# Output projection of an fp8 attention layer: weights loaded into the context's memory, chunks in alternating order

## The chip, the cores and the metric

The kernel runs on one core of a Trainium2 chip. The metric is the time of one execution on the device in microseconds (us). The engines are TensorE (PE; its weight loads are PEld), VectorE (DVE), ScalarE (ACT), GpSimd (POOL) and SyncE (SP), which here issues all transfers.

## The reference, cut to what matters

The whole model has two layers, each with an attention over a wide context, a self-attention and a feed-forward part. The change touches the last step of the first one. There, 256 tokens of width 512 make 16 heads of self-attention (`core`) and 16 heads of attention over 4096 context rows (`xout`), each head 128 wide. The 32 heads are joined, divided by a smoothing vector, clamped, rounded to fp8 and multiplied by a weight matrix of 512 x 4096:

```python
core = _gqa(q, k, v).reshape(b, s, nh * d)
...
kvx = jnp.einsum('bsi,oi->bso', cond, w_kv_x)
...
xout = _gqa(qx, kx, vx).reshape(b, s, nh * d)
cat = jnp.concatenate([core, xout], axis=-1)
catq = _div_clamp_fp8(cat, proj_smooth)
return jnp.einsum('bsi,oi->bso', catq, wproj) * (proj_in_scale * proj_w_scale)
```

The result is added to `x`.

## The kernel before

The kernel is a sequence of stages. A stage owns its memory and semaphores, and every engine has its own instruction stream in it; at its end all engines meet at a barrier (line 79), and the memory is given back. Four stages matter here.

**Self-attention** writes heads 0 to 15 of `cat`, divided and clamped but not yet rounded to fp8. Meanwhile SP loads the context `ctxT` (128 partitions x 4 x 4096 values of fp32, 8 MB in all).

**Wide cross attention** goes over eight head groups and, in each, over eight blocks of the context. TensorE projects keys and values from `ctxT` (lines 406 and 418; in the last group the values are projected late, line 418), multiplies them with the queries (431) and weighs the values (441). A semaphore `s_vp` counts the late value projections, 2 for each of the last eight blocks. When they are done nothing reads `ctxT` any more. In the last steps VectorE adds up the sums of the softmax (634 and 635), divides, clamps and rounds to fp8 (lines 615 to 624, and `fp8_round`, lines 105 to 108), and writes heads 16 to 31 of `cat`. SP loads queries and weights and moves feed-forward units early in this stage; its last instruction waits for the last of these stores (line 370).

**Output projection** (`fp8_output_stage`) takes the 32 heads as eight chunks of four heads, in order 0 to 7. For a chunk:

- SP loads the raw weights, 128 x 2048 values of fp32 (1 MB), into one of three buffers `raw` (line 694), and waits for a buffer from the fourth load on.
- ScalarE copies them into `hi`, in the format that TensorE multiplies in one pass (line 704), and VectorE subtracts: `lo = raw - hi` (line 715). Both are rings of four buffers.
- Chunks 0 to 3 (self-attention) are rounded to fp8 by VectorE in four operations, into `lhs` (`fp8_round`). Chunks 4 to 7 have been rounded in the wide stage, and ScalarE only casts them into `lhs` (line 699), all four at the start of its stream.
- TensorE runs 16 matmuls of 128 x 512: for each of four heads and two halves of the tokens one with `hi` (line 730) and one with `lo` (732), all added into two accumulators.

TensorE waits for all four casts once (`s_q`) and then, chunk by chunk, for `lo`. VectorE does, in order, rounding 0, `lo` 0, rounding 1, `lo` 1 and so on to `lo` 3, then `lo` 4 to `lo` 7, waits for all products and updates `x` in two operations (line 720). A helper `link` lets VectorE wait for the operation that it has just issued, before it goes on; `dve.sem_inc` is an increment of its own behind it.

**Layer norm and causal attention** follow. Their weights are loaded by instructions that SP issues after the barrier.

Of the kernel before, what the change touches and what calls it, by code (L numbers as in the profile page):

```python
# [14 lines left out]
F32 = mybir.dt.float32  # L15
# [4 lines left out]
ALU = mybir.AluOpType  # L20
# [3 lines left out]
P = 128  # L24
TOK = 256
NT = TOK // P
DM = 512
KC = DM // P
D = 128
# [18 lines left out]
F_TILES = [(0, 128), (128, 128), (256, 96)]  # L48
FFN_LATE = [6, 22, 5, 7, 23] + [u + n for n in range(8, 16) for u in (0, 16)]
# [235 lines left out]
def wide_cross_attention_stage(nc, C, ctxT, s_ctx, w, s_w, wkv_dram, q_dram, vecs, inv_smooth, cat, units, early):  # L285
# [22 lines left out]
    with Stage(nc, "wide") as st:  # L308
# [32 lines left out]
        with nc.Block() as block:  # L341

            @block.sync
            def _(sp):
# [25 lines left out]
                sp.wait_ge(s_stored, 16 * FFN_EARLY)  # L370

# [300 lines left out]
def fp8_output_stage(nc, cat, w_dram, wscale, x):  # L672
# [3 lines left out]
    NRAW, NSPLIT = 3, 4  # L676
    with Stage(nc, "oproj") as st:
        power = st.sb("power", [P, CH * TOK], BF16)
        shifted = st.sb("shifted", [P, CH * TOK])
        lhs = st.sb("lhs", [P, 2 * NH, TOK], F32R)  # L680
        raw = [st.sb(f"raw{i}", [P, CH, DM]) for i in range(NRAW)]
# [3 lines left out]
        s_raw = [st.sem(f"raw_loaded{i}") for i in range(NRAW)]  # L685
        s_q, s_mm, s_hi, s_lo, s_dve = (st.sem(n) for n in ("rounded", "products", "high", "low", "dve"))
        with nc.Block() as block:

            @block.sync
            def _(sp):  # L690
                for c in range(NCH):
                    if c >= NRAW:
                        sp.wait_ge(s_lo, c - NRAW + 1)
                    sp.dma_start(raw[c % NRAW][:, :, :], w_dram[c]).then_inc(s_raw[c % NRAW], 16)

            @block.scalar
            def _(act):
                for c in range(NCH // 2, NCH):
                    act.copy(lhs[:, CH * c:CH * (c + 1), :], cat[:, CH * c:CH * (c + 1), :]).then_inc(s_q, 1)
                for c in range(NCH):  # L700
                    act.wait_ge(s_raw[c % NRAW], 16 * (c // NRAW + 1))
                    if c >= NSPLIT:
                        act.wait_ge(s_mm, c - NSPLIT + 1)
                    act.copy(hi[c % NSPLIT][:, :, :], raw[c % NRAW][:, :, :]).then_inc(s_hi, 1)

            @block.vector
            def _(dve):
                link = Chain(dve, s_dve).after
                for c in range(NCH):
                    if c < NCH // 2:  # L710
                        part = cat[:, CH * c:CH * (c + 1), :].rearrange("p a b -> p (a b)")
                        fp8_round(dve, link, part, power[:, :], shifted[:, :],
                                  lhs[:, CH * c:CH * (c + 1), :].rearrange("p a b -> p (a b)"))
                    dve.wait_ge(s_hi, c + 1)
                    link(dve.tensor_tensor(lo[c % NSPLIT][:, :, :], raw[c % NRAW][:, :, :], hi[c % NSPLIT][:, :, :].bitcast(F32),
                                           ALU.subtract))
                    dve.sem_inc(s_lo, 1)
                dve.wait_ge(s_mm, NCH)
                for t in range(NT):
                    link(dve.scalar_tensor_tensor(out=x[:, t, :], in0=acc[t][:, :], scalar=wscale[:, 0:1], in1=x[:, t, :],  # L720
                                                  op0=ALU.mult, op1=ALU.add))

            @block.tensor
            def _(pe):
                pe.wait_ge(s_q, NCH // 2)
                for c in range(NCH):
                    pe.wait_ge(s_lo, c + 1)
                    for j in range(CH):
                        for t in range(NT):
                            pe.matmul(acc[t][:, :], lhs[:, CH * c + j, t * P:(t + 1) * P], hi[c % NSPLIT][:, j, :],  # L730
                                      start=(c == 0 and j == 0), stop=False)
                            mm = pe.matmul(acc[t][:, :], lhs[:, CH * c + j, t * P:(t + 1) * P], lo[c % NSPLIT][:, j, :],
# [2371 lines left out]
```

## Time and profile before

| | |
|---|---|
| median of 3 runs | 2563.33 us (2561.7 to 2565.37) |
| profiled execution | 2560.87 us |
| its span | 2559.1 us |
| instructions | 31520 |
| TensorE busy | 2279.3 us, 89% |
| VectorE busy | 1786.6 us, 70% |
| ScalarE busy | 1193.7 us, 47% |
| GpSimd busy | 587.4 us, 23% |
| the output projection in the span | 1169.04 to 1217.83 us |

The profile is of one execution; its time is the span plus 1.8 us around it. Times inside the trace count from the start of the span. A matmul row's start is measured, and its end is modelled, so the pace of matmuls is read from one start to the next. In square brackets a row says how long the engine was idle before the instruction, and what released it; "DVEq L717" is the increment behind `lo`.

### The profile page before, as it was taken

The page shows a single profiled execution, that of the slowest core. Times are in us where ns is not written, and L with a number is a line of the kernel's source. Part 1 is how long each engine was busy: PE and PEld are TensorE (multiplying, and loading weights), DVE is VectorE, ACT ScalarE, POOL GpSimd, SP SyncE. Part 2 cuts the span into 40 slices and gives each one's busy share as a digit, 9 for nine tenths or more (in the row PEclk, how much of TensorE's full clock was granted, in tenths as well). Part 3 has the DMA queues.
Part 4 walks back from the last instruction along what each step waited for, and adds up shares of the span by engine and source line. Part 5 has one row for each costly group of instructions (what it writes and reads, how often), then busy time and mean ns, then how long its engine had stood idle before and what let it go on. Part 6 is the DMA issues. An engine that isn't in the chain of part 4 may idle for free. (4 is left out here: it accounts for less than half of the span.)

```text
span 2559.1 us, 31520 instructions
## 1 busy us (share of the span) xinstructions
PE 2279.3 (89%) x11472; PEld 1554.3 (61%) x11472; DVE 1786.6 (70%) x3422; ACT 1193.7 (47%) x1924; POOL 587.4 (23%) x435
## 2 busy tenths in 40 slices
PE   3779999999999999896897989788888779899998
PEld 2556666666666666564674456555556337677876
DVE  7856887777777778876896976666767754554444
ACT  4443466666566666633332114576766853211111
POOL 7810033334233333440000003323141300000000
PEclk9889999999999999998997999999999989899999
DMA  3331100000000100003544100000000013656661
GB/s 132 116 140 46 46 25 29 9 29 9 29 25 13 29 13 17 0 1 132 193 169 188 52 21 10 1 10 1 6 5 1 21 75 144 216 206 220 230 237 66
DMA packets 47622, 186.40 MB, mean 73 GB/s; under 512 B 6064, under 2 KB 10928, under 8 KB 37232
## 3 DMA queue, kind: packets, MB, share of 16 engines
q1 hardware_dynamic: 47472, 184.43, 20.0%
q8 instruction: 91, 1.49, 0.2%
q14 instruction: 59, 0.48, 0.1%
HBM read 174.71 MB, written 9.70 MB: 72 GB/s over the span
## 5 line engine op out<-in xcount | busy, mean ns | idle before, releaser
L406 PE MATMUL wide_a<-wide_w,ctxT 128*128 128x256 f32 (+1 forms) x2048 | 437.8, 367 | 2.8 <-POOL wide_eps L375 2.8
L406 PEld LDWEIGHTS wide_a<-wide_w,ctxT 128*128 128x128 f32 x2048 | 368.5, 191 | 76.5 <-issue 35.7
L388 POOL TENSOR_TENSOR wide_sums<-wide_sums,wide_s 128x512 f32<-128x512 f32 x224 | 301.3, 1345 | 461.8 <-ACT wide_s L536 448.6
L431 PE MATMUL wide_scores<-wide_q,wide_keysT 128*128 128x512 f32 x512 | 238.4, 604 | 12.5 <-ACT wide_s L532 12.5
L441 PE MATMUL wide_o<-wide_s,wide_values 128*128 128x512 f32 x512 | 233.8, 600 | 3.5 <-ACT wide_s L536 3.5
L532 ACT COPY wide_s<-wide_scores 128x512 f32<-128x512 f32 x256 | 148.4, 585 | 175.7 <-PE wide_scores L431 173.9
L1812 DVE TENSOR_REDUCE int_peaks<-int_a 128x1 f32<-128x1024 f32 x128 | 156.1, 1222 | 91.3 <-PE int_a L1535 90.1
L1535 PE MATMUL int_a<-int_keys,int_qrows 96*128 96x512 bf16 x512 | 151.8, 394 | 55.9 <-DVE int_peaks L1812 27.9
L1687 ACT ACTIVATE int_prob<-int_a,int_shift,int_qscale 128x1024 uint8<-128x1024 f32 x128 | 155.4, 1216 | 50.6 <-PE int_a L1535 50.1
L431 PEld LDWEIGHTS wide_scores<-wide_q,wide_keysT 128*128 128x128 f32 x512 | 87.9, 189 | 148.8 <-ACT wide_s L532 87.8
L594 DVE TENSOR_TENSOR wide_top<-wide_top,wide_s 128x512 f32<-128x512 f32 x240 | 165.6, 690 | 16.1 <-ACT wide_s L532 10.4
L2268 PEld LDWEIGHTS moe_bank<-moe_xb,moe_gate_up 128*128 128x128 f32 (+1 forms) x1536 | 162.0, 183 | 8.3 <-issue 8.3
L2268 PE MATMUL moe_bank<-moe_xb,moe_gate_up 128*128 128x96 f32 (+1 forms) x1536 | 162.6, 266 | 4.3 <-issue 4.3
L441 PEld LDWEIGHTS wide_o<-wide_s,wide_values 128*128 128x128 f32 x512 | 96.7, 192 | 100.2 <-issue 93.9
L607 DVE TENSOR_TENSOR wide_s<-wide_s,wide_peak_rows 128x2048 f32<-128x2048 f32 x64 | 146.8, 2294 | 0.8
L570 DVE BATCH_NORM_STATS2 wide_stats<-wide_keys 128x6 f32<-128x128 f32 x256 | 60.6, 278 | 110.9 <-ACT wide_values L514 108.4
L1446 PE MATMUL int_vp<-int_wk,ctxT_again 128*128 128x128 f32 x1024 | 126.6, 279 | 5.2 <-PEq L79 2.2
L1446 PEld LDWEIGHTS int_vp<-int_wk,ctxT_again 128*128 128x128 f32 x1024 | 122.7, 194 | 12.3 <-issue 4.0
L512 ACT COPY wide_keys<-wide_a 128x256 f32<-128x256 f32 x128 | 46.6, 364 | 174.3 <-PE wide_a L406 174.2
L536 ACT ACTIVATE wide_s<-wide_s 128x2048 f32<-128x2048 f32 x64 | 122.4, 1912 | 5.5 <-DVE wide_s L607 4.8
L1535 PEld LDWEIGHTS int_a<-int_keys,int_qrows 96*128 96x128 bf16 x512 | 37.0, 99 | 118.8 <-DVE int_peaks L1812 49.7
L2469 DVE TENSOR_REDUCE moe_coef<-moe_misc 96x1 f32<-96x4 f32 x32 | 5.1, 158 | 137.3 <-PE moe_misc L2277 137.3
(425 smaller groups left out, 4285.7 us busy)
## 6 DMA issues: line engine op xcount, KB each, us to landing
moe_gate_up<-hbm_m_gu SPq DMA_DIRECT2D x34, 1408.0 KB, 6.2
moe_down<-hbm_m_down_a SPq DMA_DIRECT2D x34, 512.0 KB, 6.9
causal_wqkv<-hbm_wqkv SPq DMA_DIRECT2D x8, 1536.0 KB, 6.6
ctxT<-hbm_ctxT SPq DMA_DIRECT2D x4, 2048.0 KB, 15.1
oproj_raw<-hbm_wproj SPq DMA_DIRECT2D x8, 1024.0 KB, 5.0
ctxT_again<-hbm_ctxT SPq DMA_DIRECT2D x4, 2048.0 KB, 21.6
wide_unit<-hbm_ffn_units SPq DMA_DIRECT2D x27, 256.0 KB, 2.7
ffn_early<-wide_unit SPq DMA_DIRECT2D x27, 256.0 KB, 2.0
```

The lines of the kernel that those rows point to most:

```text
L388: ins = pool.tensor_tensor(sums[0][:, :], before, part[:, j, :], ALU.add)
L406: mm = pe.matmul(a[h][:, j, cols], ctxT[:, kc, t * P:(t + 1) * P], w[g % 2][:, kc, cols], start=(kc == 0), stop=(kc == KC - 1))
L431: pe.matmul(sp_[j % 2][:, :], keysT[:, j, :], q[:, :], start=True, stop=True).then_inc(s_s, 1)
L441: mm = pe.matmul(o[g % 2][:, :], values[m % VR][:, j, :], s[m % SR][:, j, :], start=(c == 0 and j == 0), stop=(c == QPG - 1 and j == 3))
L532: act.copy(s[n % SR][:, j, :], sp_[j % 2][:, :]).then_inc(s_se, 1)
L594: link(dve.tensor_tensor(top[:, :], before, s[n % SR][:, j, :], ALU.max))
L607: dve.tensor_tensor(s[m % SR][:, :, :], s[m % SR][:, :, :], peak_rows[:, :].unsqueeze(1).to_broadcast([P, 4, COLS]), ALU.subtract).then_in ...
L1446: mm = pe.matmul(vp[:, t * P:(t + 1) * P], ctxT[:, kc, i * P:(i + 1) * P], wk[:, kc, :], start=(kc == 0), stop=(kc == KC - 1))
L1535: mm = pe.matmul(wide[n % 2][:, z * 512:(z + 1) * 512], qrows[0:3 * HD, h, t * P:(t + 1) * P], keys[0:3 * HD, h % HC, j * 512:(j + 1) * 51 ...
L1687: act.activation(prob[u % 4][:, p * 1024:(p + 1) * 1024], wide[n % 2][:, :], ACT.Exp, bias=shift[:, u % NU:u % NU + 1], scale=qscale[:, t, ...
L1812: dve.tensor_reduce(peaks[u % 2][:, p:p + 1], wide[n % 2][:, :], AX.X, ALU.max).then_inc(s_ad, 1)
L2268: mm = pe.matmul(dst[0:m, j, :], wgu[i][:, kc, z * EI + f0:z * EI + f0 + m], xb[q % 2][:, kc, e % BATCH, :], start=(kc == 0), stop=(kc == ...
```

## The change

Four things are edited.

1. The weights' memory. `raw` is a view of `ctxT` with eight places of 1 MB, one for each chunk. The two buffers of the wide stage's weights are freed before the projection stage; `ctxT` stays until its end.
2. The loads. A function issues four of them with no wait between. It is called at the end of SP's stream in the wide stage, behind a wait for the last value projection (`s_vp`), and again as SP's only work in the projection stage.
3. The order of chunks is 4, 0, 5, 1, 6, 2, 7, 3; the position in this order is `n`. ScalarE's cast of a chunk stands in front of its copy to `hi`; TensorE waits for each chunk's cast (`s_cast`) or rounding (`s_q`). `lhs` is eight tiles rather than one. The rings `hi` and `lo` have three buffers rather than four.
4. The waits. `lo` and the two updates of `x` no longer go through `link`; `lo` increments its semaphore itself. Each rounding is followed by an increment of its own (`s_q`).

```diff
--- before.py
+++ after.py
@@ -46,6 +46,7 @@
 TOPG = 3
 EG = 8
 F_TILES = [(0, 128), (128, 128), (256, 96)]
+OPROJ_ORDER = [4, 0, 5, 1, 6, 2, 7, 3]
 FFN_LATE = [6, 22, 5, 7, 23] + [u + n for n in range(8, 16) for u in (0, 16)]
 FFN_EARLY_UNITS = [n for first in (0, 16, 4, 20, 32, 36, 40, 44) for n in range(first, first + 4) if n not in FFN_LATE]
 FFN_EARLY = len(FFN_EARLY_UNITS)
@@ -282,7 +283,7 @@
                     assert chain.n == PER, chain.n
 
 
-def wide_cross_attention_stage(nc, C, ctxT, s_ctx, w, s_w, wkv_dram, q_dram, vecs, inv_smooth, cat, units, early):
+def wide_cross_attention_stage(nc, C, ctxT, s_ctx, w, s_w, wkv_dram, q_dram, vecs, inv_smooth, cat, units, early, loads):
 
 
 
@@ -368,6 +369,8 @@
                         if i + 2 < FFN_EARLY:
                             load_unit(i + 2)
                 sp.wait_ge(s_stored, 16 * FFN_EARLY)
+                sp.wait_ge(s_vp, 2 * (N - LATE))
+                loads(sp)
 
             @block.gpsimd
             def _(pool):
@@ -669,68 +672,64 @@
                     put(NG - 1, piece)
 
 
-def fp8_output_stage(nc, cat, w_dram, wscale, x):
+def fp8_output_stage(nc, cat, raw, s_raw, loads, wscale, x):
 
     CH = 4
     NCH = 2 * NH // CH
-    NRAW, NSPLIT = 3, 4
+    NSPLIT = 3
     with Stage(nc, "oproj") as st:
         power = st.sb("power", [P, CH * TOK], BF16)
         shifted = st.sb("shifted", [P, CH * TOK])
-        lhs = st.sb("lhs", [P, 2 * NH, TOK], F32R)
-        raw = [st.sb(f"raw{i}", [P, CH, DM]) for i in range(NRAW)]
+        lhs = [st.sb(f"lhs{c}", [P, CH, TOK], F32R) for c in range(NCH)]
         hi = [st.sb(f"hi{i}", [P, CH, DM], F32R) for i in range(NSPLIT)]
         lo = [st.sb(f"lo{i}", [P, CH, DM], F32R) for i in range(NSPLIT)]
         acc = [st.ps(f"acc{t}", [P, DM]) for t in range(NT)]
-        s_raw = [st.sem(f"raw_loaded{i}") for i in range(NRAW)]
-        s_q, s_mm, s_hi, s_lo, s_dve = (st.sem(n) for n in ("rounded", "products", "high", "low", "dve"))
+        s_cast, s_q, s_mm, s_hi, s_lo, s_dve = (st.sem(n) for n in ("cast", "rounded", "products", "high", "low", "dve"))
         with nc.Block() as block:
 
             @block.sync
             def _(sp):
-                for c in range(NCH):
-                    if c >= NRAW:
-                        sp.wait_ge(s_lo, c - NRAW + 1)
-                    sp.dma_start(raw[c % NRAW][:, :, :], w_dram[c]).then_inc(s_raw[c % NRAW], 16)
+                loads(sp)
 
             @block.scalar
             def _(act):
-                for c in range(NCH // 2, NCH):
-                    act.copy(lhs[:, CH * c:CH * (c + 1), :], cat[:, CH * c:CH * (c + 1), :]).then_inc(s_q, 1)
-                for c in range(NCH):
-                    act.wait_ge(s_raw[c % NRAW], 16 * (c // NRAW + 1))
-                    if c >= NSPLIT:
-                        act.wait_ge(s_mm, c - NSPLIT + 1)
-                    act.copy(hi[c % NSPLIT][:, :, :], raw[c % NRAW][:, :, :]).then_inc(s_hi, 1)
+                for n, c in enumerate(OPROJ_ORDER):
+                    if c >= NCH // 2:
+                        act.copy(lhs[c][:, :, :], cat[:, CH * c:CH * (c + 1), :]).then_inc(s_cast, 1)
+                    act.wait_ge(s_raw[n], 16)
+                    if n >= NSPLIT:
+                        act.wait_ge(s_mm, n - NSPLIT + 1)
+                    act.copy(hi[n % NSPLIT][:, :, :], raw[:, n, :, :]).then_inc(s_hi, 1)
 
             @block.vector
             def _(dve):
                 link = Chain(dve, s_dve).after
-                for c in range(NCH):
+                for n, c in enumerate(OPROJ_ORDER):
                     if c < NCH // 2:
                         part = cat[:, CH * c:CH * (c + 1), :].rearrange("p a b -> p (a b)")
-                        fp8_round(dve, link, part, power[:, :], shifted[:, :],
-                                  lhs[:, CH * c:CH * (c + 1), :].rearrange("p a b -> p (a b)"))
-                    dve.wait_ge(s_hi, c + 1)
-                    link(dve.tensor_tensor(lo[c % NSPLIT][:, :, :], raw[c % NRAW][:, :, :], hi[c % NSPLIT][:, :, :].bitcast(F32),
-                                           ALU.subtract))
-                    dve.sem_inc(s_lo, 1)
+                        fp8_round(dve, link, part, power[:, :], shifted[:, :], lhs[c][:, :, :].rearrange("p a b -> p (a b)"))
+                        dve.sem_inc(s_q, 1)
+                    dve.wait_ge(s_hi, n + 1)
+                    dve.tensor_tensor(lo[n % NSPLIT][:, :, :], raw[:, n, :, :], hi[n % NSPLIT][:, :, :].bitcast(F32), ALU.subtract).then_inc(s_lo, 1)
                 dve.wait_ge(s_mm, NCH)
                 for t in range(NT):
-                    link(dve.scalar_tensor_tensor(out=x[:, t, :], in0=acc[t][:, :], scalar=wscale[:, 0:1], in1=x[:, t, :],
-                                                  op0=ALU.mult, op1=ALU.add))
+                    dve.scalar_tensor_tensor(out=x[:, t, :], in0=acc[t][:, :], scalar=wscale[:, 0:1], in1=x[:, t, :],
+                                             op0=ALU.mult, op1=ALU.add)
 
             @block.tensor
             def _(pe):
-                pe.wait_ge(s_q, NCH // 2)
-                for c in range(NCH):
-                    pe.wait_ge(s_lo, c + 1)
+                for n, c in enumerate(OPROJ_ORDER):
+                    pe.wait_ge(s_lo, n + 1)
+                    if c < NCH // 2:
+                        pe.wait_ge(s_q, n // 2 + 1)
+                    else:
+                        pe.wait_ge(s_cast, n // 2 + 1)
                     for j in range(CH):
                         for t in range(NT):
-                            pe.matmul(acc[t][:, :], lhs[:, CH * c + j, t * P:(t + 1) * P], hi[c % NSPLIT][:, j, :],
-                                      start=(c == 0 and j == 0), stop=False)
-                            mm = pe.matmul(acc[t][:, :], lhs[:, CH * c + j, t * P:(t + 1) * P], lo[c % NSPLIT][:, j, :],
-                                           start=False, stop=(c == NCH - 1 and j == CH - 1))
+                            pe.matmul(acc[t][:, :], lhs[c][:, j, t * P:(t + 1) * P], hi[n % NSPLIT][:, j, :],
+                                      start=(n == 0 and j == 0), stop=False)
+                            mm = pe.matmul(acc[t][:, :], lhs[c][:, j, t * P:(t + 1) * P], lo[n % NSPLIT][:, j, :],
+                                           start=False, stop=(n == NCH - 1 and j == CH - 1))
                     mm.then_inc(s_mm, 1)
 
 
@@ -3065,6 +3064,7 @@
         s_ctx = nc.alloc_semaphore("ctx_loaded")
         q_dram = nc.dram_tensor("cross_queries", (P, NH, TOK), F32, kind="Internal").ap()
         with ExitStack() as cross:
+            weights = cross.enter_context(ExitStack())
             with ExitStack() as inner:
                 def sbi(name, shape, dt=F32):
                     return inner.enter_context(nc.sbuf_tensor(name, shape, dt, side="right"))
@@ -3073,7 +3073,7 @@
                 v = sbi("v", [P, NT, NG * D])
                 front_stage(nc, C, A, x, A, (ln2, in_scales, scales, wscale, vecs, smooth, inv_smooth), qT, q_dram, kT, v)
                 ctxT = cross.enter_context(nc.sbuf_tensor("ctxT", [P, KC, SC], F32))
-                w = [cross.enter_context(nc.sbuf_tensor(f"wide_w{i}", [P, KC, 2 * D], F32)) for i in range(2)]
+                w = [weights.enter_context(nc.sbuf_tensor(f"wide_w{i}", [P, KC, 2 * D], F32)) for i in range(2)]
                 s_w = [nc.alloc_semaphore(f"wide_w_loaded{i}") for i in range(2)]
                 def loads(sp):
                     sp.dma_start(w[0][:, :, :], A["wkvx"][0]).then_inc(s_w[0], 16)
@@ -3081,9 +3081,20 @@
                         sp.dma_start(ctxT[:, kc, :], A["ctxT"][:, kc, :]).then_inc(s_ctx, 16)
 
                 self_attention_stage(nc, C, qT, kT, v, inv_smooth, cat, loads)
+            raw = ctxT[:, :, :].rearrange("p k n -> p (k n)").rearrange("p (c j n) -> p c j n", c=8, n=DM)
+            s_raw = [nc.alloc_semaphore(f"wproj_loaded{n}") for n in range(8)]
+
+            def projection_loads(first):
+                def loads(sp):
+                    for n in range(first, first + 4):
+                        sp.dma_start(raw[:, n, :, :], A["wproj"][OPROJ_ORDER[n]]).then_inc(s_raw[n], 16)
+
+                return loads
+
             wide_cross_attention_stage(nc, C, ctxT, s_ctx, w, s_w, A["wkvx"], q_dram, vecs, inv_smooth, cat, A["ffn_units"],
-                                       early)
-        fp8_output_stage(nc, cat, A["wproj"], wscale, x)
+                                       early, projection_loads(0))
+            weights.close()
+            fp8_output_stage(nc, cat, raw, s_raw, projection_loads(4), wscale, x)
 
 
 _OUT = "out_dram"
```

## Rows read from the trace of the kernel before

**Rows 1.** The page: busy time of TensorE; the chain that ended last, by engine.

```profile
PE 2279.3 (89%) x11472; PEld 1554.3 (61%) x11472; DVE 1786.6 (70%) x3422; ACT 1193.7 (47%) x1924; POOL 587.4 (23%) x435
...
PE 13%; DMA 0%; issue 0%; ACT 0%; DVE 0%; SPq 0%; DVEq 0%
```

**Rows 2.** Windows: length, PE, PEld, DVE, ACT, POOL busy, clock, DMA share, GB/s.

```profile
1169.00:1184.00 15.00, 5.33 (x15) 4.29 (x16) 10.85 (x10) 10.02 (x8) 0.00 (x0) 0.54 0.74 280
1184.00:1196.20 12.20, 8.32 (x35) 5.97 (x33) 11.54 (x11) 4.58 (x3) 0.00 (x0) 1.00 0.52 174
...
1200.00:1216.30 16.30, 16.25 (x72) 13.11 (x70) 5.58 (x4) 3.83 (x2) 0.00 (x0) 1.00 0.17 69
...
1169.00:1218.70 49.70, 33.68 (x128) 26.34 (x128) 33.06 (x26) 19.14 (x12) 0.00 (x0) 0.83 0.46 169
```

**Rows 3.** Timeline of ScalarE in the stage: start, length, line, tiles.

```profile
1169.06 3.89 ACT L699 CAST oproj_lhs<-cat 128x1024 fp32r<-128x1024 bf16 x4 [15.35 <-PEq L79]
1174.16 1.90 ACT L704 CAST oproj_hi<-oproj_raw 128x2048 fp32r<-128x2048 f32 x1 [1.22 <-DMA oproj_raw<-hbm_wproj]
1176.88 1.90 ACT L704 CAST oproj_hi<-oproj_raw 128x2048 fp32r<-128x2048 f32 x1 [0.82 <-DMA oproj_raw<-hbm_wproj]
```

**Rows 4.** Timeline of VectorE in the stage.

```profile
1169.09 0.43 DVE L105 TENSOR_SCALAR oproj_power<-cat 128x1024 uint16<-128x1024 uint16 x1 [1.56 <-PEq L79]
...
1176.17 2.29 DVE L715 TENSOR_TENSOR oproj_lo<-oproj_raw,oproj_hi 128x2048 fp32r<-128x2048 f32 x1 [3.67 <-ACT oproj_hi L704]
1178.61 0.43 DVE L105 TENSOR_SCALAR oproj_power<-cat 128x1024 uint16<-128x1024 uint16 x1
...
1180.79 1.22 DVE L108 TENSOR_TENSOR oproj_lhs<-oproj_shifted,oproj_power 128x1024 fp32r<-128x1024 f32 x1
1182.05 2.29 DVE L715 TENSOR_TENSOR oproj_lo<-oproj_raw,oproj_hi 128x2048 fp32r<-128x2048 f32 x1
...
1193.82 7.17 DVE L715 TENSOR_TENSOR oproj_lo<-oproj_raw,oproj_hi 128x2048 fp32r<-128x2048 f32 x3
...
1216.29 1.54 DVE L720 SCALAR_TENSOR_TENSOR x_res<-oproj_acc,wscale,x_res 128x512 f32<-128x512 f32 x2 [8.61 <-PE oproj_acc L732]
1218.80 0.69 DVE L137 BATCH_NORM_STATS2 ln_stats<-x_res 128x6 f32<-128x512 f32 x1 [0.97 <-PEq L79]
```

**Rows 5.** Timeline of TensorE in the stage: eight of 128 matmuls.

```profile
1178.67 0.76 PE L730 MATMUL oproj_acc<-oproj_hi,oproj_lhs 128*128 128x512 f32 x1 [18.59 <-DVEq L717]
...
1183.01 0.40 PE L730 MATMUL oproj_acc<-oproj_hi,oproj_lhs 128*128 128x512 f32 x1
...
1184.45 0.50 PE L730 MATMUL oproj_acc<-oproj_hi,oproj_lhs 128*128 128x512 f32 x1
...
1187.99 0.39 PE L732 MATMUL oproj_acc<-oproj_lo,oproj_lhs 128*128 128x512 f32 x1
1190.34 0.50 PE L730 MATMUL oproj_acc<-oproj_hi,oproj_lhs 128*128 128x512 f32 x1 [1.96 <-DVEq L717]
...
1196.22 0.52 PE L730 MATMUL oproj_acc<-oproj_hi,oproj_lhs 128*128 128x512 f32 x1 [1.94 <-DVEq L717]
...
1199.95 0.42 PE L732 MATMUL oproj_acc<-oproj_lo,oproj_lhs 128*128 128x512 f32 x1
...
1215.87 0.39 PE L732 MATMUL oproj_acc<-oproj_lo,oproj_lhs 128*128 128x512 f32 x1
```

**Rows 6.** Waits of SP's queue from 1100 us: total, times, longest.

```profile
SPq L341 <- PEq L341: 153.1, 1, 153.1
```

**Rows 7.** Timeline of TensorE near the wide stage's end.

```profile
1147.75 3.73 PE L418 MATMUL wide_a<-wide_w,ctxT 128*128 128x128 f32 x32
```

**Rows 8.** The transfers into raw: time from issue to landing.

```profile
DMA to landing us min/median/max: 4.7/5.0/9.4
```

**Rows 9.** Timeline of VectorE in the wide stage.

```profile
1066.57 2.28 DVE L607 TENSOR_TENSOR wide_s<-wide_s,wide_peak_rows 128x2048 f32<-128x2048 f32 x1
1068.77 2.86 DVE L594 TENSOR_TENSOR wide_top<-wide_top,wide_s 128x512 f32<-128x512 f32 x4
```

## The prediction

> **What bounds the kernel now.** I began with the page. TensorE is busy 89% of the span, and the chain that ended last accounts for 13% of the span, all of it in the expert layer at the very end [rows 1]. So neither total nor chain says anything of the output projection; that has to be read from its own stretch.
>
> The windows of the stage come next [rows 2]. The stage lasts from 1169.0 to about 1217.9 us, 49 us or 1.9% of the span; nothing better than that is at stake. TensorE is busy 5.3 of the first 15 us, 8.3 of the next 12.2, and 16.25 of 16.3 in the last stretch. VectorE is the reverse: 10.9 of 15 and 11.5 of 12.2 early, 5.6 of 16.3 late. The reader is to see a stage in which first VectorE is the limit and TensorE waits, then TensorE is the limit and VectorE waits.
>
> The three timelines tell why. ScalarE spends 3.9 us on the four casts, then waits until 1174.16 for the first weights, whose transfer was issued when the stage began [rows 3]. The subtraction that makes `lo` waits for that copy and starts at 1176.17 [rows 4]. TensorE's first matmul is at 1178.67, 9.6 us into the stage [rows 5]. Chunks 0 to 3 each need a rounding and a subtraction: on VectorE the start of the second `lo` lies behind the first by 1182.05 - 1176.17 = 5.88 us, while TensorE needs 3.54 us plus one matmul at full clock (1184.45 to 1187.99), so TensorE idles some 2 us before 1190.34 and 1196.22. From there 80 matmuls run without a gap to 1215.87, their `hi` and `lo` having been made ahead. What sets the end is therefore VectorE's pace over the first four chunks, then 20.0 us of TensorE.
>
> **The change, part by part.** *Early loads.* Four of the eight 1 MB loads move from this stage to SP's queue at the end of the wide stage, behind a new wait for the last value projections. Those matmuls end at about 1151.5 [rows 7]. SP has by then nothing in its queue: it sits 153.1 us at the end of the wide block before TensorE ends [rows 6]. Nobody is queued behind the new wait, and nobody waits for SP before the barrier. Loads of this size landed in 4.7 to 9.4 us [rows 8] and, issued together, let their casts start 1176.88 - 1174.16 = 2.7 us apart, and the first cast started 5.1 us after the stage did [rows 3], so the four land by about 1151.5 + 5.1 + 3 x 2.7 = 1164.7. The first is wanted at 1170.0. Even at 9.4 us plus 8.1 us, the last is in by 1169.0. The cost of the move is nothing; the cover is the tail of the wide stage after 1151.5, and with that cover gone the first copy to `hi` would start at 1174.16 again. The bounds for a disturbance of the wide tail are 0 and small: VectorE's 0.43 us operations of the stage cost 0.43 us both at 1169.09 and at 1178.61, transfers under way [rows 4]. I take 0.
>
> *Late loads.* The other four are issued at the stage's start, without waits for a buffer, and land between 1174.2 and 1182.3 by the same reckoning. They serve positions 4 to 7, wanted from 1184 on. With weights always there in time, what is late next is VectorE.
>
> *Order 4, 0, 5, 1, 6, 2, 7, 3.* Roundings stay four and subtractions eight, but the two kinds of chunk alternate. This is the part that moves work: the surplus of VectorE in the first half and that of TensorE in the second now lie beside each other. Also the first chunk needs no rounding and the cast in front of it is one, not four.
>
> *Chained waits.* The subtraction no longer waits for itself and no longer needs a separate increment; each rounding gets a separate increment. Before, three subtractions in a row took 7.17 us, so 2.44 us from one to the next for 2.29 us of work, a gap of 0.15; the step inside a rounding has a gap of 0.03 to 0.04 [rows 4]. The difference, 0.11 us, I charge to each rounding for its new increment (bounds 0 and 0.11). A subtraction of the same shape without a wait is in the wide stage: 1066.57 to 1068.77, 2.20 us to the next start [rows 9]. So 2.44 becomes 2.20. The bounds are 2.20 and 2.44; I take 2.20, since the row has the same shape, operation and engine. The Trainium skill (VectorE: DVE Perf Modes, The DRAIN you can't avoid) says that operations with a semaphore after each run no slower than without; by that rule the pitch would stay at 2.44 and the gain below would be some 1.7 us smaller. The trace disagrees, with 2.44 against 2.20 us [rows 4, 9].
>
> **The sum.** ScalarE: cast at 1169.06; the next can start (3.89 - 1.04)/3 = 0.95 us later, 1170.0; the copy to `hi` takes 1.90, to 1171.9. VectorE starts the first `lo` 0.11 us behind it, as it did at 1176.17 behind 1176.06: 1172.0. From there it has no other wait: seven subtractions at 2.20 (15.4), four roundings at 3.44 (1178.61 to 1182.05) plus 0.11 (14.2), the last subtraction 2.29. Together 31.9 us, so the last `lo` is ready at 1203.9.
>
> Does TensorE keep up? Its first chunk can start at 1172.0 + 2.29 + 0.11 = 1174.4. The first ten matmuls before took 4.34 us, 0.43 each, at the lower level of the clock, 1.2 GHz (the stretch to 1184 was granted 0.54 in the mean) [rows 2], then 0.227 each, 15.92 us over the 70 steps from 1199.95 to 1215.87, at 2.4 GHz [rows 5]. That gives 5.7 us for the first chunk, at worst 6.9 if all 16 are slow: end 1180.1 to 1181.3. `lo` of the following positions is ready at 1180.1, 1182.3, 1188.0, 1190.2, 1195.9, 1198.1 and 1203.9. With 3.65 us a chunk TensorE starts them at 1180.2 (or 1181.3), 1183.9, 1188.1, 1191.8, 1196.0, 1199.7 and 1204.0. It waits some 0.5 us once in each pair and is never behind when the last `lo` comes; a slow start is absorbed.
>
> The rings go from four to three. ScalarE's copy for position n now waits for TensorE's chunk n - 3. Its tightest place is position 4: chunk 1 done at 1183.9 (1184.9 at worst), copy done by 1185.9 (1186.9), wanted by VectorE at 1187.9. Margin 1.0 us at worst. Cost 0, as long as the clock is up.
>
> End: last chunk 1204.0 + 3.54 + 0.39 = 1207.9, then the two updates of `x` take 1.54 or, without the wait between, about 1.4: 1209.4. Before, it was 1216.29 + 1.54 = 1217.8. The gain is 8.4 us: about 4.1 from the earlier first weights and fewer casts, the rest from alternation and the shorter pitch. The next stage starts by a barrier behind this (1218.80 for VectorE) and issues its own loads after it, so all moves by that amount.
>
> The profiled execution took 2560.87 us, span 2559.1; less 8.4 it gives 2552.5. The median of the runs lies 2.46 us above the profiled execution, so in terms of medians the forecast is 2563.33 - 8.4 = 2554.9, say 2555.0.
>
> **Rivals.**
>
> *A, the clock falls again and again.* The matmul row at 1196.22 follows a wait of 1.94 us, and up to 1199.95 nine matmuls take 3.73 us in place of 2.05: one fall costs 1.6 us [rows 5]. But the same wait before 1190.34 cost nothing, and the waits to come are 0.5 us. If it fell once in each pair, TensorE would need 128 x 0.227 = 29.1, plus 2.1 for the slow start, 6.4 for four falls and 1 for waits: end at 1213.0, a gain of 3.3 us, 2560.0. The Trainium skill (TensorE: Matmul & The Clock Gate, A second HAM failure mode: psum-queue depth-cycling) describes a kernel whose short, frequent idles between groups of matmuls made the clock oscillate; the change puts such idles where there was one long run. Chance 0.10.
>
> *B, slower.* The same place, carried to the end: the clock stays at its lower level. TensorE works from 1174.4 and must be done by 1216.3 to break even, 41.9 us; each slow matmul adds 0.2 us to 29.1, so from 64 slow matmuls of 128 the stage loses. All 128 slow: 54.7 us, end at 1229.3, 13 us late, 2576.3. For it: the stretch to 1184 had 0.54 of the clock. Against: that rose after 4.3 us of matmuls with no other help. Chance 0.03, and 0.02 for any other loss.
>
> *C, the loads come no earlier in effect* (the wait is released late, or the transfer waits for the barrier). Then the first copy starts at 1174.16 and all lies 4.1 us later: gain 4.3, 2559.0. Against it stand the 153 us of idle SP. Chance 0.06.
>
> *D, hidden anyway or given back later*: 2563.3. The next stage's first matmuls wait for loads issued in it, not at a fixed time, so this is unlikely: 0.06.
>
> **How the numbers follow.** The forecast case has 0.73. Its own range: gain 8.4, less 1.7 if the pitch stays 2.44, less 1.6 for one uncovered fall, plus 0.4 if the increments are free: 5.1 to 8.8 us; the three runs spread 1.8 us either way. From 2563.3 - 8.8 - 1.8 = 2552.7 to 2563.3 - 5.1 + 1.8 = 2560.0, which takes in A and C too; I widen the low end to 2552.0 for a fall of the clock that the kernel before has and the new one is spared. 0.2% is 5.1 us, about what a measurement can tell from no change. Faster by more: nearly all of the forecast case, a small part of A and C: 0.78. Within: 0.17. Slower: 0.05.
>
> **What would show it.** In the new profile: SP's first four loads at 1151.5; the first `hi` at 1170.0 and first `lo` at 1172.0; first matmul at 1174.4; subtractions 2.20 us before what follows them (2.44 would be the other bound); pairs of chunks 7.95 us apart on VectorE; TensorE waiting about 0.5 us per pair with a clock of 1.0 from 1181 on; `x` updated by 1209.4. Wrong would be: ScalarE waiting for TensorE at position 4 with VectorE behind it, TensorE without idle and a clock below 0.9, or a stage whose first VectorE operation starts later than 1169.09.

## The result, and the profile after

The changed kernel takes 2549.2 us in the median of 8 runs (2544.06 to 2554.91), the kernel before, timed in the same series, 2562.51. One of the eight runs of the kernel before took 9195.4 us; it counts in that median and not in the ratio, and without it the median is 2561.7. The ratio is 0.9957, with a 95% interval of 0.9944 to 0.9971: 11.0 us faster, between 7.4 and 14.3. The forecast was 2555.0 in a range of 2552.0 to 2560.0. The direction and the place of the gain are right, the time lies below the range.

The profiled span is 2543.0 us, 16.1 less than before. Only a part of that lies in the stage that was edited. First, its timelines after the change. ScalarE:

```profile
1165.14 1.04 ACT L698 CAST oproj_lhs<-cat 128x1024 fp32r<-128x1024 bf16 x1 [15.36 <-PEq L80]
1166.10 3.69 ACT L702 CAST oproj_hi<-ctxT 128x2048 fp32r<-128x2048 f32 x2
1169.69 1.04 ACT L698 CAST oproj_lhs<-cat 128x1024 fp32r<-128x1024 bf16 x1
1170.64 1.89 ACT L702 CAST oproj_hi<-ctxT 128x2048 fp32r<-128x2048 f32 x1
...
1180.16 1.91 ACT L702 CAST oproj_hi<-ctxT 128x2048 fp32r<-128x2048 f32 x1 [1.26 <-PE oproj_acc L731]
```

The first copy to `hi` starts 0.96 us into the stage, with no wait for weights; before, it was 5.1 [rows 3]. The first four of its loads were issued in the wide stage, behind the last value projection. TensorE, then SP, whose row covers all eight loads, the first at 1147.66 and the last four from 1165.12 on:

```profile
1143.84 3.73 PE L421 MATMUL wide_a<-wide_w,ctxT 128*128 128x128 f32 x32
1147.66 19.71 SPq L3090 DMA_DIRECT2D ctxT<-hbm_wproj  x8
```

The fourth load was issued at 1148.98, and the longest of the eight took 11.0 us to land, so the first four were in by 1160.0, 6 us before they were wanted. VectorE:

```profile
1168.02 2.29 DVE L713 TENSOR_TENSOR oproj_lo<-ctxT,oproj_hi 128x2048 fp32r<-128x2048 f32 x1 [4.42 <-ACT oproj_hi L702]
1170.23 0.42 DVE L106 TENSOR_SCALAR oproj_power<-cat 128x1024 uint16<-128x1024 uint16 x1
...
1173.78 4.49 DVE L713 TENSOR_TENSOR oproj_lo<-ctxT,oproj_hi 128x2048 fp32r<-128x2048 f32 x2
1178.19 0.42 DVE L106 TENSOR_SCALAR oproj_power<-cat 128x1024 uint16<-128x1024 uint16 x1
...
1197.65 2.29 DVE L713 TENSOR_TENSOR oproj_lo<-ctxT,oproj_hi 128x2048 fp32r<-128x2048 f32 x1
1204.00 1.41 DVE L716 SCALAR_TENSOR_TENSOR x_res<-oproj_acc,wscale,x_res 128x512 f32<-128x512 f32 x2 [4.06 <-PE oproj_acc L731]
1206.14 0.69 DVE L138 BATCH_NORM_STATS2 ln_stats<-x_res 128x6 f32<-128x512 f32 x1 [0.73 <-PEq L80]
```

From 1168.02 to the end of its last subtraction VectorE waits for nothing. Two subtractions take 4.49 us, so 2.20 from one to the next, and a rounding with its increment 3.55 (1170.23 to 1173.78). TensorE, six of its matmuls:

```profile
1170.37 0.80 PE L729 MATMUL oproj_acc<-oproj_hi,oproj_lhs 128*128 128x512 f32 x1 [14.21 <-DVE oproj_lo L713]
...
1173.94 0.41 PE L729 MATMUL oproj_acc<-oproj_hi,oproj_lhs 128*128 128x512 f32 x1
...
1184.08 0.50 PE L729 MATMUL oproj_acc<-oproj_hi,oproj_lhs 128*128 128x512 f32 x1 [0.39 <-DVE oproj_lo L713]
...
1192.04 0.50 PE L729 MATMUL oproj_acc<-oproj_hi,oproj_lhs 128*128 128x512 f32 x1 [0.41 <-DVE oproj_lo L713]
...
1200.00 0.50 PE L729 MATMUL oproj_acc<-oproj_hi,oproj_lhs 128*128 128x512 f32 x1 [0.37 <-DVE oproj_lo L713]
...
1203.57 0.39 PE L731 MATMUL oproj_acc<-oproj_lo,oproj_lhs 128*128 128x512 f32 x1
```

The first matmul comes 5.2 us into the stage, not 9.6 [rows 5], and the long run of 80 matmuls has gone. The waits that are left are of 0.2 to 0.4 us, always for `lo`. Windows of the stage, with the columns of [rows 2]:

```profile
1165.10:1180.10 15.00, 9.55 (x33) 7.47 (x34) 11.76 (x10) 10.25 (x7) 0.00 (x0) 0.71 0.70 281
1180.10:1204.00 23.90, 22.69 (x96) 17.41 (x94) 19.16 (x16) 8.59 (x5) 0.00 (x0) 1.00 0.00 0
```

The clock is at 2.4 GHz (1.00) throughout the second window. From the stage's first cast to the update of `x` it is 38.86 us, before 47.23: 8.37 less. From the first cast to the layer norm's first operation it is 41.00 against 49.74: 8.74 less. So the stage explains 8.7 of the 16.1 us. The remaining 7.4 us lie elsewhere, nearly all in code that nobody edited. The wide stage's first projection starts at 192.70, in the kernel before at 195.34: 2.6 us. The wide stage takes 1.3 us less, and the quantised attention, a stage of the second layer, 3.9 us less (599.5 for 603.4). The other stages together take 0.5 us more.

### The profile page after: what moved, and what is told of

Same layout as the page of the kernel before. It is cut to its first block and busy times, and to the rows that moved or that the text cites. A ratio compares the mean times of both kernels' runs of the same rounds, so it can differ in the third digit from the quotient of the medians.

```text
span 2543.0 us, 31519 instructions
## 1 busy us (share of the span) xinstructions
PE 2271.2 (89%) x11472; PEld 1548.0 (61%) x11472; DVE 1784.9 (70%) x3422; ACT 1193.7 (47%) x1924; POOL 587.2 (23%) x435
```

## The experiments

Two theories stand against each other. R: the change is worth the 8.7 us of its stage, and the rest is the spread of runs, which three runs had shown too small. M: the change also makes other stages faster, by its memory or its timing. Beside them stands the question within the stage: which edit brought how much. Below, "stage" is the time from the stage's first ScalarE instruction to the start of the update of `x`, and "wide" that from the first wide projection to the first ScalarE instruction of the projection stage, both from each kernel's timelines. A ratio compares a kernel with runs of the kernel before in its own series. The four from `same_before` to `late_loads` are one series, `old_order` to `rounded_ahead` another, on another chip, and `tail_rounds` a third; across series ratios are compared, not medians.

| kernel | median (runs) | ratio to before, 95% interval | wide | stage |
|---|---|---|---|---|
| before | 2562.51 (8) | | 973.7 | 47.23 |
| changed | 2549.2 (8) | 0.9957, 0.9944 to 0.9971 | 972.4 | 38.86 |
| `same_before` | 2559.4 (12) | 1.0000, 0.9988 to 1.0013 | 971.9 | 47.11 |
| `same_after` | 2549.69 (10) | 0.9961, 0.9949 to 0.9972 | 972.0 | 38.82 |
| `delay` | 2560.39 (12) | 1.0003, 0.9989 to 1.0016 | 974.3 | 48.15 |
| `late_loads` | 2555.88 (12) | 0.9983, 0.9970 to 0.9995 | 974.2 | 42.72 |
| `old_order` | 2553.48 (12) | 0.9971, 0.9961 to 0.9981 | 972.1 | 41.71 |
| `chained` | 2552.08 (7) | 0.9964, 0.9949 to 0.9980 | 972.5 | 40.59 |
| `round_first` | 2546.32 (6) | 0.9948, 0.9932 to 0.9965 | 971.7 | 37.65 |
| `rounded_ahead` | 2558.27 (12) | 0.9990, 0.9976 to 1.0004 | 984.8 | 35.81 |
| `tail_rounds` | 2548.65 (6) | 0.9952, 0.9939 to 0.9966 | 973.7 | 36.45 |

**`same_after` and `same_before`**: the two kernels once more, with no edit.

> The changed kernel again, unaltered. Its stage took 38.86 us from ScalarE's first cast (1165.14) to the update of x (1204.00), 8.36 less than the kernel before (1169.06 to 1216.29); 8.74 less to the first operation of the layer norm. Theory R: only the stage's 8.7 us are the change's, the rest of the difference of the profiled spans (16.1 us) is the spread of runs; then the stage takes 38.9 us again within 0.5, the ratio tends to 0.9966, and the two profiles of the same kernel differ by some us in stages that nobody edited (self-attention, quantised attention). Rival M: the rest (2 to 7 us) comes with the change; then the ratio stays at 0.9957 or lower and the wide stage again begins 2.6 us earlier, and the quantised attention again takes 4 us less.

> The kernel before against itself. Both theories: ratio 1.0000. It measures how far two sets of runs of one kernel lie apart, and its profile how far the stages of one kernel move between executions. Theory R needs movements of 2 to 4 us in single stages and a spread of runs of some 10 us; rival M expects the stages within 1 us of the kernel before's first profile.

The stage repeats within 0.12 us in either kernel. The rest of the program does not. In the second profile of the changed kernel the first wide projection starts 2.2 us later than in the first, though not a line differs:

```profile
192.70 7.58 PE L409 MATMUL wide_a<-wide_w,ctxT 128*128 128x256 f32 x34 [2.77 <-POOL wide_eps L378]
```

```profile
194.92 5.42 PE L409 MATMUL wide_a<-wide_w,ctxT 128*128 128x256 f32 x24 [2.77 <-POOL wide_eps L378]
```

Over all eleven profiles that start lies between 192.1 and 197.4 us. The quantised attention moves more. Its first ScalarE instruction and the next stage's first matmul, in the changed kernel:

```profile
1488.62 1.28 ACT L1623 ACT_TABLE_LOAD   x1 [7.44 <-PEq L80]
...
2088.10 1.22 PE L1941 MATMUL decay_pq<-xT,decay_wkv 128*128 128x256 f32 x2 [1.85 <-DMA decay_wq<-hbm_d_wq]
```

and in `same_after`:

```profile
1488.01 1.28 ACT L1623 ACT_TABLE_LOAD   x1 [7.26 <-PEq L80]
...
2092.84 1.65 PE L1941 MATMUL decay_pq<-xT,decay_wkv 128*128 128x256 f32 x3 [1.71 <-DMA decay_wq<-hbm_d_wq]
```

That is 599.5 and 604.8 us for one and the same kernel, so the 3.9 us that this stage seemed to gain lie within its own spread. Between the two profiles of the kernel before the wide stage differs by 1.8 us and this one by 1.9. M's forecasts, that stages stay within 1 us and that the two gains come again, are wrong.

The kernel before ran from 2550.64 to 2566.31 us in 33 runs, with a median of 2560.2, where the three runs shown ahead of the prediction had 2561.7 to 2565.37. In the two later series its medians were 2559.8 (28 runs) and 2559.77 (11). What goes with the spread is TensorE's granted clock. The 45 runs of the kernel before in this series, by the mean clock of each:

```
granted clock    runs   mean us   lowest    highest
0.963 to 0.967     11    2554.8   2550.64   2559.34
0.960 to 0.962     17    2559.4   2553.30   2562.39
0.957 to 0.959     17    2562.5   2559.07   2566.31
```

One stage shows how. Self-attention in `chained` and in `late_loads`, whose code is the same in it (windows, columns as in [rows 2]):

```profile
132.00:192.00 60.00, 45.91 (x192) 34.68 (x192) 36.31 (x96) 29.02 (x84) 10.11 (x23) 0.86 0.34 145
```

```profile
132.00:192.00 60.00, 47.18 (x182) 35.86 (x183) 34.15 (x93) 28.52 (x83) 11.19 (x24) 0.78 0.35 149
```

With a granted clock of 0.86 TensorE got 192 matmuls done in these 60 us, with 0.78 only 182; the wide stage starts at 192.13 in the one and at 197.41 in the other. About 1.3 of these 5.3 us lie ahead of the stage, which begins at 130.43 and at 131.71. The two profiles of the changed kernel fit in: 0.86 and 192.70, 0.83 and 194.92. Why the clock was granted less in one execution than in another no run shows.

**`delay`**: the gain handed back inside the stage.

```diff
                 dve.wait_ge(s_mm, NCH)
+                for _ in range(4):
+                    link(dve.tensor_tensor(lo[0][:, :, :], raw[:, 0, :, :], hi[0][:, :, :].bitcast(F32), ALU.subtract))
```

> The changed kernel with four more linked subtractions (2.33 us each) on VectorE in front of the update of x, about 9.3 us of waiting and nothing else: the stage is then 0.6 us longer than in the kernel before. Theory R: ratio to the kernel before 1.0002, within its interval. Rival M: still 2 to 7 us faster, 0.9973 to 0.9992. x is the same.

```profile
1210.59 9.27 DVE L716 TENSOR_TENSOR oproj_lo<-ctxT,oproj_hi 128x2048 fp32r<-128x2048 f32 x4 [4.04 <-PE oproj_acc L733]
1219.90 1.41 DVE L718 SCALAR_TENSOR_TENSOR x_res<-oproj_acc,wscale,x_res 128x512 f32<-128x512 f32 x2
```

The insertion took 9.3 us and the ratio is 1.0003. With the stage's gain cancelled nothing of the change can be seen; the interval reaches from 2.8 us faster to 4.1 us slower. That is the clearest evidence for R: it excludes all but the lowest end (2 us, 0.9992) of what M forecast. The profiled execution of `delay` is also a warning: taken alone, its 2567.19 us lie 6 us above the profiled execution of the kernel before.

**`late_loads`**: the early loads taken back.

```diff
                 sp.wait_ge(s_stored, 16 * FFN_EARLY)
-                sp.wait_ge(s_vp, 2 * (N - LATE))
-                loads(sp)
...
-                    for n in range(first, first + 4):
+                    for n in range(8):
```

> The changed kernel with all eight loads issued at the stage's start, none in the wide stage. My account: the first copy to hi waits for its weights until 5.1 us into the stage in place of 0.96, and all behind it is 4.1 us later; the gain over the kernel before falls from 8.7 to 4.6 us (ratio 0.9982). Rival: the early loads are worth nothing, since the casts and VectorE fill that time; then the stage stays 8.7 us shorter.

```profile
1171.63 1.04 ACT L696 CAST oproj_lhs<-cat 128x1024 fp32r<-128x1024 bf16 x1 [15.36 <-PEq L80]
1176.44 1.90 ACT L700 CAST oproj_hi<-ctxT 128x2048 fp32r<-128x2048 f32 x1 [3.76 <-DMA ctxT<-hbm_wproj]
```

The copy waits 3.76 us for the transfer, and the stage takes 42.72 us, 3.86 more than the changed kernel's. The early loads are worth that.

**`old_order`**: early loads and free subtractions, but chunks 0 to 7.

```diff
-OPROJ_ORDER = [4, 0, 5, 1, 6, 2, 7, 3]
+OPROJ_ORDER = [0, 1, 2, 3, 4, 5, 6, 7]
...
-                        pe.wait_ge(s_q, n // 2 + 1)
+                        pe.wait_ge(s_q, c + 1)
...
-                        pe.wait_ge(s_cast, n // 2 + 1)
+                        pe.wait_ge(s_cast, c - NCH // 2 + 1)
```

> The changed kernel with the chunks in order 0 to 7; early loads and unchained waits stay. My account: VectorE rounds and subtracts for each of the first four chunks, 3.55 + 2.20 = 5.75 us from one lo to the next, so the first matmul is at 6.0 us of the stage and the fourth chunk can begin at 23.2; from there 80 matmuls take 18.2 us. The update of x begins 41.8 us into the stage, 43.4 if the clock falls once as in the kernel before, against 38.86: 2.9 to 4.5 us of the gain are the order's. Rival: with weights there early the order is worth under 1 us, since TensorE is the bound either way.

```profile
1180.22 0.50 PE L729 MATMUL oproj_acc<-oproj_hi,oproj_lhs 128*128 128x512 f32 x1 [0.18 <-DVE oproj_lo L713]
1185.98 0.50 PE L729 MATMUL oproj_acc<-oproj_hi,oproj_lhs 128*128 128x512 f32 x1 [1.82 <-DVE oproj_lo L713]
1191.75 0.50 PE L729 MATMUL oproj_acc<-oproj_hi,oproj_lhs 128*128 128x512 f32 x1 [1.82 <-DVE oproj_lo L713]
```

The two idles of 1.8 us are back. The stage takes 41.71 us, so the order brings 2.85 us. The clock did not fall behind these idles: the matmuls after them start 0.23 us apart. The rival, under 1 us for the order, is out.

**`chained`**: the wait and the increment back behind each `lo`.

```diff
-                    dve.tensor_tensor(lo[n % NSPLIT]...).then_inc(s_lo, 1)
+                    link(dve.tensor_tensor(lo[n % NSPLIT]...))
+                    dve.sem_inc(s_lo, 1)
```

> The changed kernel with the helper's wait and the separate increment put back behind each lo. My account: the step from a lo to what follows goes from 2.20 to 2.44 us, seven times, and VectorE sets the end: the update of x begins 1.7 us later, 40.5 us into the stage. The rule that a semaphore behind an operation costs nothing: 38.9 as before.

```profile
1173.52 4.73 DVE L713 TENSOR_TENSOR oproj_lo<-ctxT,oproj_hi 128x2048 fp32r<-128x2048 f32 x2
1178.40 0.43 DVE L106 TENSOR_SCALAR oproj_power<-cat 128x1024 uint16<-128x1024 uint16 x1
```

Two subtractions take 4.73 us and what follows starts 4.88 after the first: 2.44 each. The stage takes 40.59 us, so the free subtractions bring 1.73 us, seven times 0.25. `chained` puts two things back at once, the wait for the operation itself and the increment of its own; in the changed kernel `lo` still raises a semaphore, and goes at 2.20. The rule of the Trainium skill (VectorE: DVE Perf Modes, The DRAIN you can't avoid) that a semaphore after each operation costs nothing fits that increment, and not the pair that `chained` puts back. The rows part the pair: in a rounding, where only the wait stands between two operations, the next one starts 0.03 to 0.04 us after the end of the last, behind a free `lo` it starts 0.09 us before the end shown (2.20 for 2.29), and a separate increment adds 0.11 us (3.55 for 3.44). By this estimate the wait costs about 0.13 us and the increment 0.11.

Each taken from the changed kernel alone, the early loads, the order and the free subtractions bring 3.86 + 2.85 + 1.73 = 8.44 us, and the whole stage gained 8.37: little is left for the casts and the rings.

**`round_first`**: chunk 0 rounded while VectorE waits for the first `hi`.

```diff
...
+                round_chunk(0)
                 for n, c in enumerate(OPROJ_ORDER):
-                    if c < NCH // 2:
...
+                    if 0 < c < NCH // 2:
+                        round_chunk(c)
```

> The changed kernel with chunk 0 rounded at the very start, in the time in which VectorE waits for the first hi. My account: first lo 3.55 us into the stage in place of 2.9, so the first matmul is 0.7 us later; but VectorE has 3.55 us less on the rest, and TensorE becomes the bound: 6.0 + 29.1 + 2.1 (slow start) + 0.4 = 37.6, 1.3 us less than 38.86. Rival: the ring of three stalls ScalarE and the end stays at 38.9.

The stage takes 37.65 us, 1.21 less than the changed kernel's. TensorE is now the limit: its first matmul is 5.93 us into the stage, and from there it runs without a wait. The ring of three does make ScalarE and behind it VectorE wait, by 0.4 and 1.3 us, but does not stall TensorE.

**`rounded_ahead`**: all of self-attention's heads rounded in the wide stage.

```diff
                 for n in range(N + LAG + 1):
+                    if n % QPG == 6:
+                        e = n // QPG
+                        if e < NG:
+                            own = cat[:, 2 * e:2 * e + 2, :].rearrange("p h n -> p (h n)")
+                            fp8_round(dve, link, own, power[:, :], out[:, :], own)
...
-                    if c >= NCH // 2:
-                        act.copy(lhs[c][:, :, :], cat[:, CH * c:CH * (c + 1), :]).then_inc(s_cast, 1)
...
+                    act.copy(lhs[c][:, :, :], cat[:, CH * c:CH * (c + 1), :]).then_inc(s_cast, 1)
...
```

> The changed kernel with the first 16 heads rounded in the wide stage, two heads each in eight of VectorE's gaps (in place, 2.1 us each), only casts left for ScalarE, and the copy to hi ahead of the cast. My account: VectorE has only the eight subtractions, the first lo is at 2.0 us and the first matmul at 4.4 us of the stage; TensorE is the bound: 4.4 + 29.1 + 2.1 + 0.4 = 36.0, 2.9 us less than 38.86, and the wide stage, bound by TensorE, costs nothing. Rival: the eight roundings of 2.1 us delay what TensorE waits for in the wide stage, up to 2 us each, and the kernel is slower than the changed one by up to 13 us.

The stage gains what was expected, 35.81 us, and the wide stage pays for it: 984.8 us against 971.7 to 974.3 in all others, 1.5 us for each of the eight roundings. My account failed there. VectorE in the middle of the wide stage:

```profile
612.13 0.61 DVE L106 TENSOR_SCALAR wide_power<-cat 128x512 uint16<-128x512 uint16 x1
612.77 1.31 DVE L107 TENSOR_SCALAR wide_power<-wide_power 128x512 bf16<-128x512 bf16 x1
614.11 1.70 DVE L108 TENSOR_TENSOR wide_out<-cat,wide_power 128x512 f32<-128x512 bf16 x1
615.85 0.69 DVE L109 TENSOR_TENSOR cat<-wide_out,wide_power 128x512 bf16<-128x512 f32 x1
616.58 0.48 DVE L573 BATCH_NORM_STATS2 wide_stats<-wide_keys 128x6 f32<-128x128 f32 x2
```

GpSimd at the same time:

```profile
609.53 5.74 POOL L391 TENSOR_TENSOR wide_sums<-wide_sums,wide_s 128x512 f32<-128x512 f32 x4 [8.67 <-ACT wide_s L539]
```

The rounding took 4.4 us, not 2.1, and the statistics of the next keys stand behind it. The three stretched operations lie beside GpSimd's additions (609.53 to 615.27) and the last one, at its usual 0.69, does not. The first of the eight roundings is the control: it comes before GpSimd's first addition and takes 2.0 us. Its second operation:

```profile
270.25 0.29 DVE L107 TENSOR_SCALAR wide_power<-wide_power 128x512 bf16<-128x512 bf16 x1
```

Six of the others took 4.4 us and the last, beside GpSimd throughout, 6.1. The Trainium skill (SBUF — State Buffer, Who interferes with whom) names such a conflict of VectorE with GpSimd over a shared port; the trace agrees, with 1.31 us for an operation of 0.29. On TensorE the delay shows as idle time in the wide stage, in the changed kernel and then in `rounded_ahead`:

```profile
PE wide_scores L434 <- ACT wide_s L535: 12.5, 15, 3.1
```

```profile
PE wide_scores L434 <- ACT wide_s L535: 20.9, 19, 3.1
```

That is 8.4 of the 12 us; the rest was not traced. Whether roundings of 2.1 us in these gaps would have been free was not tried.

**`tail_rounds`**: chunk 0 alone, in the two gaps at the wide stage's very end, and the copy to `hi` ahead of the cast.

```diff
+                    if n >= N + LAG - 1:
+                        e = n - (N + LAG - 1)
+                        own = cat[:, 2 * e:2 * e + 2, :].rearrange("p h n -> p (h n)")
+                        fp8_round(dve, link, own, power[:, :], out[:, :], own)
                     if n - LAG >= (NG - 1) * QPG and n - LAG < N:
                         add(n - LAG)
...
-                    if c >= NCH // 2:
+                    if c == 0 or c >= NCH // 2:
...
```

> The changed kernel with chunk 0 rounded in place in the two gaps that VectorE has in the last two steps of the wide stage (3.24 and 4.01 us idle in the trace, 2.1 us of rounding put into each), its cast left to ScalarE, and each copy to hi ahead of the cast. My account: both gaps end with a wait for something else, so the wide stage keeps its length (its first projection to the next stage's first instruction 972 to 974 us in seven profiles); the first matmul is at 4.4 us of the stage, and TensorE sets the end at 4.4 + 29.1 + 2.1 + 0.4 = 36.0, 2.9 us less than 38.86. Ratio to the kernel before 0.9955. Rival: work in VectorE's gaps is paid in full, as the eight roundings cost 12 us in rounded_ahead; then the wide stage is 4 us longer and the kernel 1 us slower than the changed one, 0.9970.

```profile
1158.38 0.69 DVE L109 TENSOR_TENSOR cat<-wide_out,wide_power 128x512 bf16<-128x512 f32 x1
1159.77 3.36 DVE L618 RECIPROCAL wide_out<-wide_rows 128x512 f32<-128x512 f32 x1 [0.69 <-PE wide_rows L479]
```

VectorE still waits 0.69 us for the sums after the second rounding, and waits 1.08 us after the first, so neither delays what follows it; wide, at 973.7 us, lies within the 971.7 to 974.3 of the other kernels. The stage takes 36.45 us, 0.5 more than expected and 2.4 less than the changed kernel's. The excess lies in the first chunk, which took 6.3 us for 5.8 in the changed kernel: twelve of its matmuls went at the slow pace of 0.43 us, not eight. Of the versions that leave the wide stage alone or nearly so, this one has the shortest projection stage; in runs it cannot be told from the changed kernel or from `round_first`, whose intervals overlap its own.

## Why the prediction was right in the stage and wrong in the range

- *Early loads land in time, at no cost*: right. SP issued them from 1147.66 on, as the last value projection ended, and wide is no longer with them (972.4 and 972.0) than without (974.2 in `late_loads`). I put 4.1 us on the first copy's earlier start, fewer casts included; `late_loads` measured 3.86.
- *The order* makes VectorE's pace the limit throughout: right. It waited for nothing after 1168.02. `old_order` took 41.71 us for a forecast of 41.8.
- *2.44 becomes 2.20, and 0.11 us for each rounding's increment*: right, 2.20 and 3.55 us; `chained` confirms the price. The sentence that the trace disagrees with the rule on semaphores went too far: the 2.44 us hold a wait and a separate increment, the 2.20 an increment on the operation itself.
- *TensorE keeps up, the ring of three costs nothing*: right; the first chunk took 5.75 us for 5.7. That a slow start is absorbed shows in `delay`: its first chunk took 6.55 us, and its last matmul began 38.42 us into the stage, as in the changed kernel (38.43).
- *The end*: 38.86 us from the stage's start, for 1207.9 - 1169.06 = 38.8. The two updates and the way to the layer norm gave 0.37 us more (1.41 for 1.54 us, then 0.73 us of waiting for 0.97), so the stage's gain is 8.74 for 8.4.
- *Rival A and B*, the clock: it stayed at 1.00 from 1180 on. *Rival C* is what `late_loads` builds: 4.3 us of gain forecast, 47.23 - 42.72 = 4.5 measured. *Rival D*, a gain hidden or given back later, is refuted by the ratio of the changed kernel; `delay` adds that time in this stage reaches the end: its 9.3 us moved the ratio from 0.9961 (`same_after`) to 1.0003, which is 10.8 us, with intervals of some 3 us either way.
- *What failed* is the step "the three runs spread 1.8 us either way", and with it the base of 2563.33. The kernel before spreads 8 us either way, and its median over 33 runs is 2560.2. The changed kernel's 8 runs spread over 10.9 us, and their median fell 2.8 us under the range. Of the 5.8 us between forecast (2555.0) and median (2549.2) the base accounts for 3.1 us (2563.33 less 2560.2) and the stage's larger gain for 0.3; the remaining 2.3 or so are the spread of eight runs or the remainder below, and no run parts the two. That the profiled execution (2560.87) lay below all three runs was a sign of this spread, and the prediction made nothing of it. It widened the low end instead for a fall of the clock that the new kernel is spared; but that fall lies before the 1216.29 from which the gain of 8.4 us was reckoned, and was counted already.

Open is a small remainder. Seven of the nine ratios of changed kernels lie 1 to 3.4 us below what their stage times give (0.9957 for 0.9966, `round_first` 0.9948 for 0.9961), each within its interval; `delay` and `late_loads` lie within 0.5 us of it. Four of the seven were compared with the same 28 runs of the kernel before, so they are not four witnesses. An effect of 1 or 2 us outside the stage is neither shown nor excluded.

## What to carry to other kernels

Where one engine is the limit in a stage's first half and another in its second, alternate the two kinds of work before making either faster; read both timelines and lay the surpluses side by side. Memory whose last reader ends before the stage does can take the next stage's first loads, and the price of being late is read from the first wait for a transfer. For an effect below 0.5%, read the edited stage in the trace, where it repeats to 0.1 us, and take the spread of the whole program from many runs, not from three.

## What the runs showed of the hardware

An idle of 1.8 us on TensorE did not lower the clock in `old_order`, twice, and one of 1.96 us in the kernel before did not, while the next one there, of 1.94 us, did [rows 5]. `same_before` fell at the same place, behind 1.97 us:

```profile
1194.96 0.51 PE L730 MATMUL oproj_acc<-oproj_hi,oproj_lhs 128*128 128x512 f32 x1 [1.97 <-DVEq L717]
1195.30 0.60 PE L732 MATMUL oproj_acc<-oproj_lo,oproj_lhs 128*128 128x512 f32 x1
1195.70 0.63 PE L730 MATMUL oproj_acc<-oproj_hi,oproj_lhs 128*128 128x512 f32 x1
```

So idles of nearly one length cost 1.6 us or nothing, the same in both executions. In one series of a program of 2.56 ms, executions of one kernel differed by up to 15.7 us, and those with the lower mean granted clock were the longer ones. A VectorE operation of 0.29 us took 1.31 us beside GpSimd's additions.
